# Low terms of UL made by GpSimd instead of VectorE, and the second product's low terms of tile 0 placed behind the high terms of tile 1

## The reference

```
xg    = group_norm(x, 32 groups)                      # no scale or shift
w     = qkv_w @ xg                                    # 384 x 384 product over 1024 pixels: "first product"
s     = sum over the 32 channels of a head of (w / ||w over the pixels||)^2
Pi    = softmax over the 12 heads of s * temp         # per pixel and head
Pi_n  = Pi / (sum over the pixels of Pi + 1e-8)
dots  = sum over the pixels of Pi_n * w * w
u     = -(w * Pi) / (1 + dots)
y     = x + out_w @ u + out_b                         # 384 x 384 product: "second product"
```

## Time and profile before

| what | value |
|---|---|
| time, median of 3 runs | 867.71 us (867.59 to 868.12) |
| span of the profiled execution, first to last instruction | 864.9 us |
| what lies around the span, median less span | 2.8 us |
| PE busy | 851.6 us, 98% |
| DVE busy | 750.2 us, 87% |
| ACT busy | 528.3 us, 61% |
| POOL busy | 232.6 us, 27% |
| DMA | 157.42 MB, mean 182 GB/s |

### The profile page before, as it was taken

One profiled execution on the slowest core, in us unless ns is written; L12 is line 12 of the kernel. 1 busy time (PEld: TensorE's weight loads), 2 busy tenths in 40 slices (PEclk: granted clock), 3 DMA queues, 4 the chain that ended last, 5 costly groups with the idle time before them and its releaser, 6 DMA issues.

```text
span 864.9 us, 14022 instructions
## 1 busy us (share of the span) xinstructions
PE 851.6 (98%) x4290; PEld 677.7 (78%) x4290; DVE 750.2 (87%) x1396; ACT 528.3 (61%) x680; POOL 232.6 (27%) x106
## 2 busy tenths in 40 slices
PE   7999999999999999999999999999999999999997
PEld 6767788777787777787777787777887777887776
DVE  7989889898888888888888898888898888898777
ACT  3567656567555677556676556676565675566642
POOL 2432123332123331133331233321233321233300
PEclk9999999999999999999999999999999999999999
DMA  7324665544664544664535654445655446645225
GB/s 279 119 79 153 225 229 185 185 148 169 225 227 161 197 146 181 226 223 160 180 150 198 228 213 168 163 145 220 227 186 196 141 163 225 228 175 186 88 86 197
DMA packets 45259, 157.42 MB, mean 182 GB/s; under 512 B 19866, under 2 KB 23962, under 8 KB 37274
## 3 DMA queue, kind: packets, MB, share of 16 engines
q1 hardware_dynamic: 36856, 154.10, 48.5%
q10 hardware_dynamic: 8354, 2.85, 1.3%
HBM read 104.47 MB, written 52.45 MB: 181 GB/s over the span
## 4 chain that ended last, share of the span: by engine, by line
PE 92%; DVE 4%; issue 1%; DMA 1%; ACT 1%; DVEq 0%; ACTq 0%
PE acc L678 86%; PE spread_ps L800 5%; DVE stats L906 1%; DVE WS L1041 1%; DMA PIB<-pi 0%; DMA X<-in_x 0%; DVE WV L1101 0%; DVE X L1149 0%; PE acc L655 0%; DVE WS L1080 0%; ACT WS L501 0%; DMA pi<-PIT 0%; DVE X L1116 0%; ACT WV L512 0%; PE spread_ps L815 0%
## 5 line engine op out<-in xcount | busy, mean ns | idle before, releaser
L424 POOL TENSOR_TENSOR XL<-XN,XH 128x1024 fp32r<-128x1024 f32 x93 | 222.9, 2414 | 571.7 <-ACT XH L529 548.2
L501 ACT ACTIVATE WS<-acc 128x1024 f32<-128x1024 f32 x96 | 98.4, 1026 | 240.5 <-PE acc L678 197.1
L678 PE MATMUL acc<-XH,W1H 128*128 128x512 f32 x574 | 177.3, 390 | 0.1
L678 PE MATMUL acc<-XH,W1L 128*128 128x512 f32 x574 | 176.8, 389 | 0.0
L678 PE MATMUL acc<-UH,W2H 128*128 128x512 f32 x558 | 172.6, 390 | 1.3 <-ACT WV L512 1.2
L678 PE MATMUL acc<-UH,W2L 128*128 128x512 f32 x558 | 172.3, 390 | 0.0
L678 PE MATMUL acc<-XL,W1H 128*128 128x512 f32 x576 | 146.2, 389 | 0.0
L678 PE MATMUL acc<-UL,W2H 128*128 128x512 f32 x558 | 145.3, 396 | 0.0
L1149 DVE SCALAR_TENSOR_TENSOR X<-acc,bias,X 128x1024 f32<-128x1024 f32 x93 | 116.3, 1276 | 31.0 <-PE acc L678 31.0
L678 PEld LDWEIGHTS acc<-UL,W2H 128*128 128x128 f32 x558 | 102.3, 188 | 32.2 <-issue 11.9
L678 PEld LDWEIGHTS acc<-XL,W1H 128*128 128x128 f32 x576 | 108.0, 188 | 22.7 <-POOL XL L434 0.3
(11 more groups left out here) (119 smaller groups left out, 501.3 us busy)
## 6 DMA issues: line engine op xcount, KB each, us to landing
PIB<-pi SPq DMA_DIRECT2D x94, 528.0 KB, 5.1
X<-in_x SPq DMA_DIRECT2D x31, 1536.0 KB, 6.3
out_y<-X SPq DMA_DIRECT2D x30, 1536.0 KB, 6.5
gathered<-stats_rows ACTq DMA_DIRECT2D x28, 72.0 KB, 5.1
pi<-PIT SPq DMA_DIRECT2D x94, 16.5 KB
X<-in_x SPq DMA_DIRECT2D x3, 512.0 KB, 4.7
out_y<-X SPq DMA_DIRECT2D x1, 1024.0 KB, 6.0
out_y<-X SPq DMA_DIRECT2D x2, 512.0 KB, 2.6
```

The costliest lines, as they stand in the source:

```text
L424: pool.tensor_tensor(XL[:, t, :], XN[:, t, :], XH[:, t, :].bitcast(F32), ALU.subtract).then_inc(xl_done, 1)
L501: act.activation(square_tile(i, t), acc[:, t, :], ACT.Square, accum_out=sumsq[:, t:t + 1]).then_inc(squared, 1)
L678: last = pe.matmul(out[:, h * BANK:(h + 1) * BANK], w[:, k, m * P:(m + 1) * P], r[:, k, h * BANK:(h + 1) * BANK], start=(n == 0 and k == 0 ...
```

## The change

For all images but the first and the last (steps i = 2 to 31, UL of image i-1), `u_lo` is taken out of DVE's step and put at the head of POOL's step, before its three XL. In the steps up to i = 30, PE's second product is cut in high and low terms: high terms of tile 0, `head_sums(i)`, high terms of tile 1, low terms of tile 0, low terms of tile 1, then tile 2 as before. The last such step (i = 31, `late`) keeps PE's old order. For the first and the last image DVE still makes UL. The number of matmuls stays.

```diff
+            def u_lo(j, t):                                        # on POOL
+                pool.wait_ge(uh_done, j.counts(T, t + 1))
+                wait_weighed(pool, j, t)
+                pool.wait_ge(m2_done, j.counts(T))
+                pool.tensor_tensor(UL[:, t, :], w_tile(j, t), UH[:, t, :].bitcast(F32),
+                                   ALU.subtract).then_inc(ul_done[t], 1)
             def step(i):
+                if i.follows(2) and has(i):
+                    for t in range(T):
+                        u_lo(i - 1, t)
                 for t in range(T):
                     x_lo(i + 1, t)
...
+            def second_high(j, t):
+                pe.wait_ge(squared, (j + 1).counts(T, t + 1))
+                pe.wait_ge(w_kept, (j + 1).counts(T, t + 1))
+                for k in range(T):
+                    if t == 0:
+                        pe.wait_ge(uh_done, j.counts(T, k + 1))
+                    for n in (0, 1):
+                        term(acc[:, t, :], t, (W2H, W2L), (UH, UL), n, k)
+            def second_low(j, t):
+                for k in range(T):
+                    if t == 0:
+                        pe.wait_ge(ul_done[k], j.counts(1, 1))
+                    last = term(acc[:, t, :], t, (W2H, W2L), (UH, UL), 2, k)
+                last.then_inc(m2_done, 1)
...
-                second_product(i - 1, 0, {(1, 2) if late else (2, 0): lambda: head_sums(i)})
-                second_product(i - 1, 1, {(1, 2): lambda: spread_heads(i), (2, 1): lambda: spread_totals(i)} if late else {})
-                second_product(i - 1, 2, {})
+                if late:
...
+                    return
+                second_high(i - 1, 0)
+                head_sums(i)
+                second_high(i - 1, 1)
+                second_low(i - 1, 0)
+                second_low(i - 1, 1)
+                second_high(i - 1, 2)
+                second_low(i - 1, 2)
...
                 weigh(i - 1, 2)
-                u_lo(i - 1, 0)
-                u_lo(i - 1, 1)
                 group_moments(i + 1)
                 head_sum_weights(i)
                 group_norm(i + 1)
-                u_lo(i - 1, 2)
                 group_stats(i + 2, [0])
```

More of the change, by code:

```diff
@@ L826, in step @@
                 first_product(i, 2)
-                second_product(i - 1, 0, {(1, 2) if late else (2, 0): lambda: head_sums(i)})
-                second_product(i - 1, 1, {(1, 2): lambda: spread_heads(i), (2, 1): lambda: spread_totals(i)} if late else {})
-                second_product(i - 1, 2, {})
+                if late:
+                    second_product(i - 1, 0, {(1, 2): lambda: head_sums(i)})
+                    second_product(i - 1, 1, {(1, 2): lambda: spread_heads(i), (2, 1): lambda: spread_totals(i)})
+                    second_product(i - 1, 2, {})
+                    return
[6 more added lines that the diff above has]
+                second_low(i - 1, 2)
             pe.wait_ge(consts_loaded, 32)
@@ L1131, in u_lo @@
             def u_lo(j, t):
[L1133 to L1142, removed]
+                dve.wait_ge(uh_done, j.counts(T, t + 1))
+                wait_weighed(dve, j, t)
+                if final(j):
+                    dve.wait_ge(m1_done, j.counts(T, T))
+                high, low = u_tiles(j)
+                dve.tensor_tensor(low[:, t, :], w_tile(j, t), high[:, t, :].bitcast(F32),
+                                  ALU.subtract).then_inc(ul_done[t], 1)
             def finish(j, t):
```

## The result

The changed kernel takes 921.99 us (median of 4 runs, 920.77 to 923.36) against 867.65 us before; the ratio is 1.0625, 95% interval 1.0609 to 1.064. That is 54.3 us slower. The forecast was 937.2 us in a range of 866.8 to 942.0, with a chance of 0.63 for slower.

What follows compares the result with a forecast made beforehand. PE was taken to bound the loop, unbroken at 26.15 us an image. Waits of 28 x 2.26 + 3.8 + 2.4 = 69.5 us took the span from 864.9 to 934.4, plus 2.8 around it: 937.2 us, range 866.8 to 942.

Steps and rivals of the forecast that it cites:

- Part 1: Three UL leave DVE, 3.7 us of its work a step: worth 0; at most 0.74 us once, in step 2.
- Part 2: Three UL come to POOL and end before XL starts, so its queue holds back nobody: 0.
- Part 3: Tile 0's low terms move behind tile 1's high terms on PE: 0, at most 3 us for waits behind the head sums.
- Part 4: UL on POOL and DVE instructions hold each other, delaying headsum: PE waits 2.26 us a step.
- rival B: Nobody is held, or harmlessly, so PE stays unbroken: no change, 867.5 us, chance 0.34.
- the 2.26 us a step: PE's forecast wait before the head sums, started at 418.91 instead of 416.65, counted for 28 steps.
- Step 2 and step 31: The two end steps, with the same hold before the head sums: forecast 3.8 us and 2.4 us.
- A: Forecast's own case: DVE held by UL on POOL, headsum late; 937.2 us, own range 925 to 942, chance 0.54.
- rival C: DVE is held, but the weighing does not hold POOL: PE waits 1.6 us a step, 916 us, chance 0.05.
- B's second variant: Only two-input instructions are held, not L990; L996 ends at 416.29 between two UL, PE can start 416.48: 867.5 us.
- slack of 0.45 us: How much later headsum can come in the loop without harm to PE: 416.46 instead of 416.01.
- D: Only the added waits on PE cost: up to 3 us, 870.5 us, chance 0.04.

Runs made afterwards that it cites:

- d: Changed kernel with both rows of inv in PSUM from image 2 on, UL still on GpSimd: 866.99 us, ratio 0.9993 to the kernel before.
- a_pe_order: Changed kernel with UL back on VectorE at its old places, so only TensorE's new order remains: 867.48 us, ratio 0.9996.
- h: Changed kernel with the tensor_scalar on 128x3 split into three on 128x1, all in SBUF: 914.0 us, ratio 1.0524.
- b: Changed kernel with TensorE's old order, UL still on GpSimd: 922.94 us, ratio 1.0641.
- k: Changed kernel, but UL of tile 0 on GpSimd waits until all three tiles are weighed: 931.8 us, ratio 1.0744.
- f: Changed kernel with only the first row of inv (floored) in PSUM, headsum still reading two SBUF tiles: 906.09 us, ratio 1.0466.
- e: Changed kernel with only the reciprocal's row of inv in PSUM, so headsum reads one SBUF tile: 870.49 us, ratio 1.003.
- c: Changed kernel, but UL of tile 2 on GpSimd also waits until headsum is written: 870.43 us, ratio 1.0034.

## Why the prediction came out right, and where its sum was too high

**What bounds the kernel.** Right: PE's busy time did not fall for DVE's relief, and where nothing is held (d) the kernel stays at 867 us.

**Part 1, three UL off DVE: 0.** Right by itself. In d, PE in step 2 starts the head sums at 76.80 where it was 76.67: the bound of 0.74 us was not to be had, as DVE then waited for the squares until 75.66, only 0.2 us less than before, and headsum started 0.36 us after the reciprocal had ended. But the relief of DVE also moved the weighing earlier against the squares, and that made the hold of part 4 shorter, as shown below.

**Part 2, three UL on GpSimd hold back no XL: 0.** Right: with the same load d loses nothing.

**Part 3, the move of the low terms: 0.** Right by a_pe_order, with an interval of 0.1% either way. The upper bound of 3 us was not needed.

**Part 4, the hold.** The mechanism was right in each link: the weighing holds GpSimd until it ends, UL ends 2.27 us later, L990 is held by UL of tile 1 and L996 by UL of tile 2, to its end. This rested on one disturbed XL of 93 and on symmetry; the runs show the other half of it, VectorE held by GpSimd. The Trainium skill, SBUF — State Buffer, section "Who interferes with whom", says that a VectorE instruction with two SBUF inputs contends with a GpSimd instruction that reads SBUF, and that the first holds the shared ports for the whole instruction. The runs agree: 2.17 us beside a UL of 2.37, 1.08 beside one of 1.29, 0.26 with one input in PSUM. For L990, the section "What auto-detection actually checks" of VectorE: DVE Perf Modes (Trainium skill) was what spoke for the forecast and against rival B; the 0.40 us on three elements, with equal source and destination in SBUF, agree with it. For one element, where no dimension is larger than one, that section states nothing; h shows no hold.

**The term that was mis-sized is the 2.26 us a step.** Measured are 1.68 us (27.83 us a period as the mean from 109.53 to 860.92, less 26.15), so 47 us and not 63 for the 28 steps. I had carried the times of the step before over unchanged. Three things moved, here for the step at 432 to 443 us. First, the weighing now ends 4.25 us before L1027 (440.27 - 436.02), where the old rows have 3.95, which is 0.3 us off the hold. It comes with the relief of DVE and not with the hold, as d, where nothing is held, has 4.26 (415.49 - 411.23); the likely reason, not tested, is that the dots no longer wait for the softmax rows (0.4 us over the span in the page, 8.1 us before in the waits). Second, UL of tile 2 ends 6.94 us after the weighing and not 7.07 as I had added up, and a held headsum ends 0.12 us behind it, not 0.26: 0.27 us. Third, PE starts 0.13 us after headsum, not 0.19: 0.06 us; this comes with the new order, as b with the old one has 0.20 (443.48 - 443.28). Together 0.63 us, which makes 2.26 to 1.63, and this step shows 27.80 - 26.15 = 1.65.

**Step 2 and step 31.** Forecast 3.8 and 2.4 us; the head sums start 3.5 us late in step 2 (80.17 for 76.67), and step 31 adds 2.0 (27.67 us from the head sums before, where it was 25.70). What I had not foreseen is in the last section: in both steps PE also ran slower for a while, at a cost of 3.1 us in all. So the sum is 47.0 + 3.5 + 2.0 + 3.1 = 55.6 us, and the span grew by 55.5.

**The range held by luck.** The forecast's own case, A, had 925 to 942 us, and 921.99 lies below it. My allowance downwards was 12 us, for a GpSimd that lets go early; the terms that moved were others and made 16. Only because the stated range also had to take in rival B, near 867.5 us, does it hold the measured time. The signs were off in the same way: a period of 27.8 us and not 28.4, PE at 93% and not 91%. By the period and the time alone rival C (27.7 us, 916 us) was nearer than A. What speaks for A is UL of tile 0, which takes 3.34 us where C wants 2.4, and experiment k.

**The rivals.** B's second variant, that headsum slips between two UL if L990 is not held, was tried in f: it happens in a third of the steps. So L990's small hold of 0.24 us in the changed kernel is what makes it lose always. B's harmless case exists too, as e: the hold of L990 alone stays within the slack of 0.45 us in all steps of the loop but one. C and D were refuted by k and a.

**A version that beats both** was not found. d, with the operands in PSUM, is level with before, as it must be while PE is unbroken.

## What to carry to other kernels

Before moving an elementwise operation from VectorE to GpSimd, list what VectorE will run at the same time. In these runs the instruction with two SBUF inputs (headsum) and the tensor_scalar of three elements from SBUF to SBUF waited for the end of the GpSimd instruction that they met, however short they were themselves. A reciprocal of three elements in SBUF, a batch-norm aggregate, a tensor_scalar of one element, and the same instructions with one operand in PSUM did not. What counts is not the work moved but how much slack the shortest such instruction has: here 0.26 us of work with 0.45 us of slack cost 54 us. Three cures are in the runs, cheapest first: an operand in PSUM (nothing lost), a wait that puts GpSimd's instruction behind the critical one (0.3% left), shorter GpSimd instructions (half of the loss left). The relief of VectorE itself bought nothing in any of them, as TensorE sets the end.

## What was not expected

PE's granted clock fell twice inside the changed kernel, each time after PE had waited for headsum. PE had idled for 4.16 us in front of the head sums of step 2, and for 1.92 in step 31; these two stretches, windows of the changed kernel (start and end, length, busy times, then granted clock):

```profile
80.17:82.96 2.79, 2.79 (x25) 1.09 (x25) 1.91 (x5) 1.76 (x2) 0.00 (x0) 0.50 0.03 6
888.60:890.95 2.35, 2.35 (x25) 0.94 (x25) 0.00 (x0) 0.00 (x0) 0.00 (x0) 0.61 0.00 0
```

In the first the clock is at half, so at 1.2 and not 2.4 GHz, and the 24 matmuls take 2.79 instead of 1.50 us. In the 28 steps between, PE idles for 1.55 to 2.20 us each time and the head sums stay at 1.50 us. Idle time alone does not tell them apart: the clock stayed up after the 2.20 us in front of 610.74 and fell after the 1.92 of step 31. Nor does it between kernels. In both c and e PE waits 2.6 us for headsum in step 2. In c the head sums then take 1.50 us at the full clock (first line, its timeline), in e they take 2.38 us at a granted clock of 0.60 (second line, its chain of waits):

```profile
78.78 1.50 PE L831 MATMUL spread_ps<-WS,headsum 128*32 128x256 f32 x24 [2.61 <-DVE headsum L1035]
78.73 2.38 PE spread_ps L829 x24
```

This pair also gives the price: from the head sums of step 2 to those of step 3 it is 26.15 us in c and 27.74 in e, 1.6 us more. In the changed kernel the same stretch is 29.36 us where the next ones are 27.8, and from the head sums of step 31 to the end it is 31.80 us where it was 30.25. So about 3 of the 54 us are the clock's. What makes it fall in one execution and not in the other is open.

Also unexpected was how little decides in f. Its headsum comes at 129.33 in one step, when UL of tile 2 has started at about 129.25, and waits for all of it; coming 0.15 us earlier, as in the step at 103.18, it is done in 0.26 us.
